# Variance 1 of the last first columns by transposed blocks on VectorE, two links of the last chain joined, and the first group's epilogue one pair ahead

## The reference

```python
def layer_norm(x):
    mu = jnp.mean(x, axis=-1, keepdims=True)
    sigma = jnp.sqrt(jnp.mean((x - mu) ** 2, axis=-1, keepdims=True))
    return (x - mu) / sigma

x1, x2 = (x[:, :F], x[:, F:])                      # F = 5120
h1 = leaky_relu(layer_norm(x1 @ W1.T))             # W1 256 x 5120, leak 0.05
h2 = leaky_relu(layer_norm(x2 @ W1.T))
h1 = leaky_relu(layer_norm(h1 @ W2.T))             # W2 64 x 256
h2 = leaky_relu(layer_norm(h2 @ W2.T))
h = leaky_relu(layer_norm(jnp.concatenate([h1, h2], axis=-1) @ W3.T))   # W3 8 x 128
return h @ W4.T                                    # W4 1 x 8
```

## Time and profile before

| | |
|---|---|
| median of 3 runs | 232.28 us (231.49 to 232.99) |
| profiled execution | 232.81 us, span 231.0 us |
| TensorE matmuls busy | 224.3 us, 97% of the span |
| VectorE busy | 191.1 us, 83% |
| ScalarE busy | 151.7 us, 66% |
| GpSimd busy | 28.8 us, 12% |

### The profile page before, as it was taken

One profiled execution on the slowest core, in us unless ns is written; L12 is line 12 of the kernel. 1 busy time (PEld: TensorE's weight loads), 2 busy tenths in 40 slices (PEclk: granted clock), 3 DMA queues, 4 the chain that ended last, 5 costly groups with the idle time before them and its releaser, 6 DMA issues.

```text
span 231.0 us, 2894 instructions
## 1 busy us (share of the span) xinstructions
PE 224.3 (97%) x999; PEld 179.2 (78%) x999; DVE 191.1 (83%) x245; ACT 151.7 (66%) x240; POOL 28.8 (12%) x41
## 2 busy tenths in 40 slices
PE   8999999999999999999999999999999999999991
PEld 3678776888888888888878888888888878888771
DVE  4589999968869999996669699999989699979324
ACT  5797989779498598963688363665546484824630
POOL 0000020020200200000012243237001400000014
PEclk9999999999999999999999999999999999999996
DMA  6999999999999999556738958668776414150000
GB/s 201 390 407 403 378 318 281 335 289 348 319 234 348 276 295 301 184 166 226 275 65 235 296 176 269 220 208 224 246 246 245 139 74 131 53 182 1 3 0 1
DMA packets 17950, 51.93 MB, mean 225 GB/s; under 512 B 2772, under 2 KB 3156, under 8 KB 17936
## 3 DMA queue, kind: packets, MB, share of 16 engines
q1 hardware_dynamic: 15920, 48.60, 61.5%
q0 software_dynamic: 1872, 2.89, 7.7%
q10 hardware_dynamic: 144, 0.26, 0.3%
HBM read 50.95 MB, written 0.01 MB: 221 GB/s over the span
## 4 chain that ended last, share of the span: by engine, by line
PE 82%; DMA 5%; DVE 4%; ACT 4%; issue 1%; POOL 1%; SPq 1%; POOLq 0%; DVEq 0%
PE acc L1006 79%; DMA xe_raw<-x 5%; PE acc L1128 2%; DVE xe_lo L705 2%; ACT xe_hi L587 2%; ACT unused L541 1%; DVE x_sum L760 1%; PE acc L1141 1%; ACT xt_hi L587 1%; DVE x_sum L770 1%; ACT we_hi L547 0%; POOL inv L484 0%; ACT stage L547 0%; PE acc L1149 0%; PE acc L1157 0%
## 5 line engine op out<-in xcount | busy, mean ns | idle before, releaser
L1006 PE MATMUL acc<-xe_lo,we_hi 128*128 128x512 f32 x176 | 68.9, 391 | 0.3 <-DVE xe_lo L705 0.2
L1006 PE MATMUL acc<-xe_hi,we_lo 128*128 128x512 f32 x176 | 68.6, 390 | 0.0
L705 DVE TENSOR_TENSOR xe_lo<-xe_raw,xe_hi 128x1024 fp32r<-128x1024 f32 (+1 forms) x48 | 55.5, 1177 | 14.5 <-ACT xe_hi L587 14.5
L587 ACT CAST xe_hi<-xe_raw 128x1024 fp32r<-128x1024 f32 (+1 forms) x48 | 47.9, 1010 | 29.5 <-PE acc L1006 22.1
L1006 PE MATMUL acc<-xe_hi,we_hi 128*128 128x512 f32 x176 | 48.3, 391 | 0.0
L1006 PEld LDWEIGHTS acc<-xe_lo,we_hi 128*128 128x128 f32 x176 | 33.1, 188 | 8.4 <-issue 1.7
L1006 PEld LDWEIGHTS acc<-xe_hi,we_hi 128*128 128x128 f32 x176 | 32.9, 188 | 7.4 <-issue 0.7
L1006 PEld LDWEIGHTS acc<-xe_hi,we_lo 128*128 128x128 f32 x176 | 33.1, 188 | 6.7
L587 ACT CAST xt_hi<-x_sum 128x2048 fp32r<-128x2048 f32 x14 | 26.8, 1911 | 12.7 <-DVE x_sum L776 12.7
L705 DVE TENSOR_TENSOR xt_lo<-x_sum,xt_hi 128x2048 fp32r<-128x2048 f32 x14 | 32.0, 2288 | 1.9 <-ACT xt_hi L587 1.9
L1006 PE MATMUL acc<-xt_lo,ws_hi 128*128 128x512 f32 x64 | 25.0, 391 | 0.1
(11 more groups left out here) (107 smaller groups left out, 274.1 us busy)
## 6 DMA issues: line engine op xcount, KB each, us to landing
xe_raw<-x SPq DMA_DIRECT2D x51, 512.0 KB, 5.0
xs_raw<-x SPq DMA_DIRECT2D x14, 768.0 KB, 5.8
stage<-w SPq DMA_DIRECT2D x21, 256.0 KB, 5.8
x_sum<-x SPq DMA_DIRECT2D x10, 256.0 KB, 3.9
x_sum<-x SPq DMA_DIRECT2D x4, 512.0 KB, 4.2
x_sum<-x POOLq DMA_DIRECT2D x4, 512.0 KB, 8.8
stage<-w SPq DMA_DIRECT2D x2, 128.0 KB, 3.1
xe_raw<-x ACTq DMA_DIRECT2D x1, 256.0 KB, 3.2
```

Source lines behind the costliest of these rows:

```text
L587: act.copy(hi_of(u, part), raw_of(u, part)).then_inc(hi_ready[part.buffer], 1)
L705: dve.tensor_tensor(lo_of(u, part), raw_of(u, part), hi_of(u, part).bitcast(F32), ALU.subtract)\
L1006: return pe.matmul(acc[:, bank, :], w, x, start=first, stop=True, skip_group_check=True)
```

## The change

First, the b = 0 columns of the last group: `sum_variance1(g, 0)` is taken off TensorE. VectorE instead transposes the summed squares in 32x32 blocks, sums each block's rows, brings the four groups of 32 partitions side by side, and sums these into the four partition groups of `var1`. Second, `variance2` has one product in place of two, with `cancelled` = inverse times variance made ahead; and in `layer3` square and sum are one instruction for each of the tiles. Third, `first_end` is at `SEVEN + 4`.

```diff
             def variance1(n, a, b, summed):
                 dve.wait_ge(var1_summed, n)
                 dve.reciprocal(var1_inverse[:, a * J:b * J], summed)
                 dve.tensor_copy(var1[:, a * J:b * J], summed).then_inc(var1_copied, 1)
                 dve.wait_ge(var1_copied, n)
+                cancel(a, b)
+
+            def cancel(a, b):
+
+                dve.tensor_tensor(cancelled[:, a * J:b * J], var1_inverse[:, a * J:b * J], var1[:, a * J:b * J], ALU.mult)\
+                    .then_inc(cancelled_ready, 1)
+
+            def variance1_of_first_columns():
+
+                turned = h1[0][1]
+                dve.wait_ge(sq1_summed, B * (GROUPS - 1) + 1)
+                step(dve.transpose(turned, sq1_sum[0]))
+                step(dve.tensor_reduce(quarter_sums[:], turned.rearrange("p (n f) -> p n f", f=Q32), AX.X, ALU.add))
+                for q in range(4):
+                    ins = dve.tensor_copy(side_by_side[:, :, q], quarter_sums[q * Q32:(q + 1) * Q32, :])
+                step(ins)
+                for q in range(4):
+                    rows = side_by_side[:].rearrange("p (h t r) q -> p h t r q", h=H, t=T)[:, :, :, q, :]
+                    ins = dve.tensor_reduce(var1[q * Q32:(q + 1) * Q32, 0:J].rearrange("p (t h) -> p h t", t=T), rows,
+                                            AX.X, ALU.add)
+                step(ins)
+                step(dve.reciprocal(var1_inverse[:, 0:J], var1[:, 0:J]))
+                cancel(0, 1)
 
             def variance2(n, a, b, summed):
-                step(dve.tensor_tensor(var2[:, a * J:b * J], summed, var1_inverse[:, a * J:b * J], ALU.mult))
-                dve.tensor_tensor(var12[:, a * J:b * J], var2[:, a * J:b * J], var1[:, a * J:b * J], ALU.mult)\
+                dve.wait_ge(cancelled_ready, n)
+                dve.tensor_tensor(var12[:, a * J:b * J], summed, cancelled[:, a * J:b * J], ALU.mult)\
                     .then_inc(var12_ready, 1)
...
-                step(dve.scalar_tensor_tensor(out=sq3[:, t], in0=h3[:, t], scalar=1.0 / N3, in1=h3[:, t],
-                                              op0=ALU.mult, op1=ALU.mult))
-                dve.tensor_reduce(var3[:, t], sq3[:, t], AX.X, ALU.add).then_inc(var3_ready, 1)
+                for k in range(a * T, b * T):
+                    ins = dve.scalar_tensor_tensor(out=sq3[:, k], in0=h3[:, k], scalar=1.0 / N3, in1=h3[:, k],
+                                                   op0=ALU.mult, op1=ALU.mult, accum_out=var3[:, k:k + 1])
+                ins.then_inc(var3_ready, 1)
...
-                first_end = n.nth == SEVEN + 5
+                first_end = n.nth == SEVEN + 4
                 if first_end:
                     dve.wait_ge(rows_landed, 16 * (B * T + H))
                     step(dve.reciprocal(var1_inverse[:], var1[:]))
+                    cancel(0, B)
                     dve.wait_ge(small_copied, 1)
-                    variance2(B, 0, B, small[:, 0:B * J])
+                    variance2(1, 0, B, small[:, 0:B * J])
...
             sum_squares(g, 0)
-            variance1(1, 0, 1, var1_ps(g, 0, 1))
+            variance1_of_first_columns()
             sum_last_squares()
             dve.wait_ge(var2_summed, 1)
             variance2(2, 0, 1, var2_ps(g, 0, 1))
-            variance1(2, 1, 2, var1_ps(g, 1, 2))
+            variance1(1, 1, 2, var1_ps(g, 1, 2))
...
                     if m == 0:
                         layer2(u.g, 0, range(M))
-                        sum_variance1(u.g, 0)
```

More of the change, by code:

```diff
@@ L30 @@
 LEAK = 0.05
+Q32 = 32
 WARM_UP = 9
@@ L206, in rec_kernel @@
         var1_inverse = sb("var1_inverse", [P, B * J])
-        var2 = sb("var2", [P, B * J])
+        cancelled = sb("cancelled", [P, B * J])
+        quarter_sums = sb("quarter_sums", [P, NC // Q32])
+        side_by_side = sb("side_by_side", [Q32, NC // Q32, 4])
         var12 = sb("var12", [P, B * J])
@@ L282, in rec_kernel @@
         var1_copied = sem("var1_copied")
+        cancelled_ready = sem("cancelled_ready")
         small_copied = sem("small_copied")
```

## The result

| | before | after |
|---|---|---|
| median | 231.53 us of 12 runs (231.37 to 232.99) | 230.00 us of 12 runs (229.67 to 231.34) |
| ratio after to before | | 0.9927, interval 0.9911 to 0.9944 |
| profiled execution | 232.81 us, span 231.0 | 229.74 us, span 228.0 |

The changed kernel is 0.7% faster, 1.5 us by the medians and 1.7 us by the ratio, where 1.33 us were forecast. Its 230.00 us lie just under the range's low end, 230.1 us. The same kernel before, which stood at 232.28 us in the three runs that the prediction went by, has a median of 231.53 us over twelve (those three among them), and of 231.6 us over all 73 executions that this study made of it.

A forecast was written before the change was run, and what follows sets the result against it. TensorE was taken as the bound, with a chain of small results handed between engines at the end. -0.92 - 0.19 + 0.07 - 0.29 = -1.33 us from 232.28 gave 230.95 us, range 230.1 to 232.3.

The forecast's parts named there:

- The median of the three runs is 232.28, and gives 230.95.: Whole kernel: level of three earlier runs, 232.28 us, with the summed change of -1.33 us gives 230.95 us.
- -0.92 for TensorE: Last unit: without the first half's variance matmuls, layer 1 resumes at 218.30 in place of 219.22, 0.92 us less.
- Hidden on VectorE: Last unit: VectorE's replacement chain takes 3.32 us in a 4.05 us window, ends 0.7 us early and costs nothing.
- -0.19 for the joined product: End chain, second variance: one product with `cancelled` in place of two saves 0.19 us.
- +0.07 for square and sum: Layer 3 at the end: summed-output instructions become four with reads, 0.45 us against 0.38; bounds -0.11 and +0.30.
- my lower bound of -0.11: Layer 3's square and sum: if the summed output is free, the pair lasts 0.27 us, 0.11 less.
- -0.29 for the move: Middle, first reloaded weights: the epilogue one pair earlier ends TensorE's wait for ws_lo, 0.29 us less.
- no wait near 181: Rival, middle: the moved block makes TensorE wait, its spare time at 181.08 being 0.6 us; 231.5 us, chance 0.08.
- no lateness of L833: Rival, end: VectorE's window is too short, the last sums of squares 0.9 us late; 231.85 us, chance 0.1.
- no slower mechanism: Rival, end: strided reads and partition-group moves double VectorE's chain to 6.64 us; 233.55 us, chance 0.06.
- the small loads: Middle: GpSimd's small DMAs for the epilogue land by 164.9, 2.2 us before the moved block starts; no wait.

The follow-up runs named there:

- a_variance_on_tensor: The changed kernel with variance 1 of the last group's first columns back on TensorE; 230.91 us (10 runs), end 11.01 us.
- b_epilogue_moved: The kernel before with only the first group's epilogue moved one seven earlier; 231.26 us (10 runs), ratio to before 0.9989.
- a_square_apart: The changed kernel with layer 3's square and sum as two instructions again; 230.22 us (6 runs), end 10.27 us.
- a_epilogue_earlier: The changed kernel with the first group's epilogue one seven earlier still; 235.46 us (2 runs), ratio to before 1.0164.

## Why the prediction came out as it did

The mechanism held in all parts but one, the accumulator; the time fell 0.1 us out of the range because of the level it was counted from. Of the 0.95 us between 230.95 and 230.00, 232.28 - 231.53 = 0.75 are the level and 0.20 the size of the change, 1.53 by the medians against 1.33. Step by step:

- *"The median of the three runs is 232.28, and gives 230.95."* This is the step that failed. The kernel before has a median of 231.6 us over 73 executions; two of the three runs at hand lay 0.7 and 1.4 us above it. Only 15 of the 73 took 232.28 us or more, so three runs with such a median were bad luck. What differs between the traces of this study, one for each kernel and two of the changed one, is the start: the steady part began between 33.4 and 35.0 us, and the first transfer on the chain took from 4.2 to 5.9 us where it is the one that starts at 2.1. The trace of before, with 5.90 and 34.99, was the latest of all. Without the 1.51 us between its start and the changed kernel's, its 232.81 us would be 231.30, among the quicker ones of the 73 (231.15 to 233.78). That the start is what varies could not be read from a single trace; that three runs lay 1.5 us apart could. Why the first transfers land earlier or later stays open, and that the start explains the untraced executions too is likely and not shown. From 231.6 the same sum gives 230.27, inside the range. The range, with 0.85 us below the forecast, was also made of the cases and hardly of that spread.
- *-0.92 for TensorE.* Measured -0.86 to -0.87 (a_variance_on_tensor, and the chain's pieces 4.87 against 4.00). Layer 1 resumes 1.01 us after the second layer's start, as worked out from the middle of the kernel; the twelve matmuls behind it take 219.31 - 216.41 = 2.90 us where they took 222.07 - 219.22 = 2.85.
- *Hidden on VectorE.* The chain was 3.3 us against 3.32 forecast, with the transpose at 0.71 (0.69 taken, bound 2.29), the reduction at 0.69 and the eight small ones at 0.18 and 0.17 each. Idle ahead of L833: 0.72 us, forecast 0.7. The true room is 1.1 us.
- *-0.19 for the joined product.* From the product's start to the power's: 225.88 - 225.44 = 0.44 before, 222.93 - 222.69 = 0.24 after. `cancelled` of the second columns was ready at 222.58, and the second variance's matmuls at 222.57: covered, with nothing to spare; the chain in fact runs through it. No run undoes this edit alone. By subtraction, b_epilogue_moved's end (11.31) less that of a_variance_on_tensor (11.01) is 0.30 us for this edit and the next, and less the 0.12 of a_square_apart 0.18 is left for this one.
- *+0.07 for square and sum.* The term that was mis-sized, by 0.19 us and with the wrong sign: it is -0.12. There are four instructions, but a read of the accumulator starts together with the next square, so it takes no slot. The value is just past my lower bound of -0.11. The Trainium skill's statement that such an instruction is two ("VectorE: DVE Perf Modes", Two Vector instructions with no wait between them) is borne out; that it would save nothing was my reading of it, and wrong.
- *-0.29 for the move.* -0.31 by the two traces, -0.30 alone in the kernel before, and 0.48 when undone. The weight load comes 0.45 us behind the raw products, even sooner than the 0.54 of the later pair that the prediction went by. The block was shorter than forecast, 170.75 - 165.49 = 5.26 us against 6.4, since GpSimd's first power took 1.67 in place of 2.52 us there and the four squares with their reads took hardly more than the two instructions (0.45 us from 168.50, against 0.41). It took 2.52 again in `b_epilogue_moved`, with the same middle; the move doesn't hang on it.
- *The sum* by the measured parts: -0.87 - 0.20 - 0.12 - 0.31 = -1.50 us, against -1.33. The 0.17 between them is the accumulator's 0.19, with 0.05 the other way from TensorE and 0.03 from the two others.

The rivals: no wait near 181, no lateness of L833, no slower mechanism. The one nearest to life was the small loads, and a_epilogue_earlier shows how near: one seven earlier costs 5.6 us in the middle.

## What to carry to other kernels

When a matmul chain is the bound and an elementwise engine idles beside it, a small reduction over partitions is worth moving off TensorE even if it takes three times as long on the other engine (3.3 us against 1.0 here); the room is the idle time of the engine plus the wait of whoever uses the result, and repeating the new instruction finds it out. Compare such kernels by the length of stretches inside the trace, not by the whole time, when the start varies by more than the change. And take the level that a forecast is counted from out of as many executions as there are, and put their spread into the range.

## What the hardware showed that was not expected

- A VectorE instruction with a summed output is followed by a 0.08 us read of the accumulator that overlaps with the next instruction: two squares of 128x8 with their sums end 0.26 us after the first one's start, against 0.38 us for a square and a reduction.
- Four copies of 32x16 take 0.40 us when they read one group of 32 partitions and 0.72 us when each reads another.
- The block transpose of 128x512 float32 takes 0.71 us, nearly as little as the sum of the squares (0.69) and the reduction (0.69) over as many values.
- GpSimd's first power of 128x8 took 2.52 us in six kernels' traces and 1.67 us in others that differ little from them (1.67 in the changed kernel, 2.52 with its epilogue moved back). Why stays open.
